# Attention scores computed in four token groups, one quarter of the TensorE array's columns each

## The chip, the core and the metric

The kernel runs on one core of one Trainium2 chip. A core has a matrix engine (TensorE, in the profile PE for matmuls and PEld for the loads of its stationary operand), a vector engine (VectorE, DVE), a scalar engine (ScalarE, ACT), GpSimd (POOL) and a queue that issues DMAs (SyncE, SP). They run at the same time and wait for each other by semaphores. Matmul results go to PSUM, which has eight banks of 512 fp32 numbers on each of 128 partitions. The metric is the device time of one execution in microseconds (us), lower is better.

## The reference, cut to what matters

The program is a recommendation tower. `r_x` (1024 tokens of 2048 numbers) goes through two encoders, and each gives four states of 512 numbers for a token. The change lies in the complex attention over these four states:

```python
B, IN, HID, D, N, OUT = (4096, 2048, 2048, 512, 4, 512)   # H = 8 heads, HD = 64
sr = enc(er_W1, ...)          # (tokens, N, D): layer norm, gelu, two matmuls
si = enc(ei_W1, ...)
qr = heads(sr @ Wq_r.T + bq_r);  qi = heads(si @ Wq_i.T + bq_i)
kr = heads(sr @ Wk_r.T + bk_r);  ki = heads(si @ Wk_i.T + bk_i)
vr = heads(sr @ Wv_r.T + bv_r);  vi = heads(si @ Wv_i.T + bv_i)
ar = einsum('bhnd,bhmd->bhnm', qr, kr) + einsum('bhnd,bhmd->bhnm', qi, ki)
ai = einsum('bhnd,bhmd->bhnm', qi, kr) - einsum('bhnd,bhmd->bhnm', qr, ki)
mag = sqrt(ar ** 2 + ai ** 2 + 1e-08) * HD ** (-0.5)
w = softmax(mag, axis=-1)
out_r = einsum('bhnm,bhmd->bhnd', w, vr) ...
out_i = einsum('bhnm,bhmd->bhnd', w, vi) ...
attn_r = out_r @ Wo_r.T + bo_r;  attn_i = out_i @ Wo_i.T + bo_i
```

So every token has, for each of the 8 heads, a 4 x 4 table of scores between its own four states, and nothing between one token and another. Behind it come an interaction, a measurement and a small MLP.

## The kernel before

Three large parts follow each other: the first layers of both encoders (to about 713 us of the profiled span), their second layers (to about 1397 us), and `phase_states`, which has the attention (about 1399 to 2330 us) and then the rest to the end.

The attention works on 16 blocks (`NB`) of 64 tokens (`BT`). A block has C = 256 columns, 4 states times 64 tokens, kept as NG = 2 groups of 128 columns; a group is 4 states (n) times GB = 32 tokens (b). The 8 heads are taken in KD = 4 pairs, index `m`; a pair has two heads `h`. For every `m` of a block, called a step below, these pieces are issued:

- `project` (PE): queries and keys, 48 matmuls 128x256 in a split of three products (lines 53 to 55).
- `q_evac` (ACT) and `k_evac` (DVE): copy them out of PSUM, with biases, into `qs` and `ks`. `ks` holds two parts, so that one matmul gives both `ar` and `ai`.
- `score` (PE, L2041): for each head and group one fp32 matmul, stationary `qs` of 128 columns, moving `ks` of 2 x 128 columns. Its result is 128 x 128 for `ar` and for `ai`: all pairs of the 32 tokens, of which only the pairs within one token are wanted. The trace has two load records and two matmul records for each fp32 matmul. The head `h` has its own PSUM bank.
- `t_square` (ACT, L1315): squares of a bank, 512 columns, once per head.
- `pick` (DVE, L1629, L1634, L1638): adds the squares of `ar` and `ai`, multiplies by `g.mask` (1 where the tokens agree), and sums over the tokens, which leaves 16 numbers per partition.
- `t_magnitude`, `shift`, `exponent`, `total`: the softmax, once a block.
- `spread` (DVE, L1668): writes the weights back into a 128 x 128 table that is zero between different tokens, `pd`, one for each of the GH = 4 pairs of head and group.
- `t_turn` (PE, L2051) transposes `pd`, `pt_evac` (ACT, L1321) copies the result to `ptl`, and `mix` (PE, L2062) multiplies it with the values; `o_high` and `o_low` read the mix.

Each engine's order is written out by hand in its own `block_body`. The softmax of a block is used one block later: in block b, PE issues for each `m` from 1 to 3 `project(b, m)`, `t_turn(b-1, m-1)`, `score(b, m-1)`, `mix(b-1, m-1)`. Thus `score` stands between the transposes and the mix, and ACT's `pt_evac` runs while PE does `score`. The last turn, score and mix of a block stand among the matmuls for the values, and `project_out` (lines 53 to 55 again, from `t_ohi`) follows. Blocks 0 and 1 are written out, 2 to 14 run in a loop on each engine, 15 is written out.

Of the kernel before, what the change touches and what calls it, by code (L numbers as in the profile page):

```python
# [9 lines left out]
ACT = mybir.ActivationFunctionType  # L10
ALU = mybir.AluOpType
# [16 lines left out]
GB = P // N  # L28
KI = IN // P
# [889 lines left out]
def phase_states(nc, g):  # L919
# [4 lines left out]
    GH = NG * 2  # L924
    NP = 8 * KD
# [9 lines left out]
    with s.ctx:  # L935
# [15 lines left out]
        sq = sb_t("sq", [P, 2, W])  # L951
        m2 = sb_t("m2", [P, W])
# [62 lines left out]
        scored = s.sem("t_scored")  # L1015
        t_squared = s.sem("t_squared")
# [282 lines left out]
        def _(act):  # L1299
            def q_evac(b, m):  # L1300
                if not isinstance(b, int) or 4 * b + m >= 2:
                    act.wait_ge(scored, b * 8 + (2 * m - 2))
# [7 lines left out]
            def t_square(b, m):  # L1310
                for h in range(2):
                    act.wait_ge(scored, b * 8 + (2 * m + h + 1))
                    if not isinstance(b, int) or 4 * b + m >= 1:
                        act.wait_ge(t_summed, b * 4 + m)
                    act.activation(sq[:, h, :], b_sc[:, h, :], ACT.Square).then_inc(t_squared, 1)  # L1315

            def pt_evac(b, m):
# [3 lines left out]
                act.activation(ptl[:, m % 2, :], pm(b, m), ACT.Copy).then_inc(pt_read, 1)  # L1321
# [290 lines left out]
        def _(dve):  # L1612
            def k_evac(b, m):
                if not isinstance(b, int) or 4 * b + m >= 2:
                    dve.wait_ge(scored, b * 8 + (2 * m - 2))
# [7 lines left out]
            def pick(b, m):  # L1623

                dve.wait_ge(t_squared, b * 8 + (2 * m + 2))
                if not isinstance(b, int) or 4 * b + m >= 1:
                    dve.wait_ge(picked, b * 4 + m)
                sqv = sq[:, :, :].rearrange("p h (a c) -> p a h c", a=2)
                dve.tensor_tensor(m2[:, :].rearrange("p (h c) -> p h c", h=2), sqv[:, 0], sqv[:, 1], ALU.add).then_inc(t_summed, 1)  # L1629

                sqv = m2[:, :].rearrange("p (g c) -> p g c", g=GH)
                mask = g.mask[:, :, :].rearrange("p n b -> p (n b)").unsqueeze(1).to_broadcast([P, GH, P])
                dve.wait_ge(t_summed, b * 4 + (m + 1))
                dve.tensor_tensor(sqv, sqv, mask, ALU.mult).then_inc(stepped, 1)  # L1634
                dve.wait_ge(stepped, b * 6 + (m + 1))
                if not isinstance(b, int) or b >= 1:
                    dve.wait_ge(t_mag_done, b)
                dve.tensor_reduce(mg2[:, m, :, :].rearrange("p g n -> p (g n)"),  # L1638
                                  m2[:, :].rearrange("p (x b) -> p x b", b=GB), AX.X, ALU.add).then_inc(picked, 1)
# [23 lines left out]
            def spread(b, m):  # L1663
# [3 lines left out]
                for x in range(GH):  # L1667
                    ins = dve.scalar_tensor_tensor(  # L1668
                        out=pd[:, x, :, :], in0=ex[:, m, x, :].unsqueeze(2).to_broadcast([P, N, GB]),
                        scalar=tinv[:, m, x:x + 1], in1=g.mask[:, :, :], op0=ALU.mult, op1=ALU.mult)  # L1670
# [33 lines left out]

            def block_body(b, first):
# [682 lines left out]
```

## Time and profile before

| | us |
|---|---|
| median of 3 runs (2923.43 to 2924.65) | 2924.25 |
| the profiled execution's own time | 2926.15 |
| its span | 2924.4 |
| PE busy | 2812.8 |
| PEld busy | 2433.5 |
| DVE busy | 2105.9 |
| ACT busy | 1326.4 |

The profiled execution is 1.9 us longer than the median, and its span leaves 1.75 us of it outside. Busy times of different engines overlap and don't add up. A PE record lasts longer than its share of the engine, since matmuls are pipelined: the distance from one record's start to the next is what a matmul costs in a row of them. Where the trace merges records, as "x8", the time shown runs from the first start to the last end.

### The profile page before, as it was taken

To read this page: it belongs to the slowest core of one execution; us is meant where nothing else is said; L and a number is where in the kernel's file an instruction comes from. 1 tells how busy PE (TensorE), PEld (TensorE's weight loads), DVE (VectorE), ACT (ScalarE), POOL (GpSimd) and SP (SyncE) were. 2 spreads that over 40 slices of the span, in tenths; PEclk is the share of its full clock that TensorE was granted. 3 is DMA by queue.
4 is the path that set the end of the run, shared out by engine and by line. 5 is a ranking of instruction groups with operands and counts; after the bars stand their busy time and mean duration, and the time that the engine had idled before them with its cause. 6 is when DMAs were issued, how large, how long until landed. Compare 5 with 4: busy or idle time off the path is not lost. (4 is left out here: it accounts for less than half of the span.)

```text
span 2924.4 us, 41074 instructions
## 1 busy us (share of the span) xinstructions
PE 2812.8 (96%) x15040; PEld 2433.5 (83%) x15040; DVE 2105.9 (72%) x3170; ACT 1326.4 (45%) x2000; POOL 140.1 (5%) x177
## 2 busy tenths in 40 slices
PE   8999999998999999999899999999999899999797
PEld 6888888887788877888899999999999877778686
DVE  5787778763658756688677667667766759999863
ACT  2232432243533244434455555555554655555543
POOL 1000000001001010010000001000000000000000
PEclk9999999999999999999999999999999999999899
DMA  6555565535737776378422322232223463344310
GB/s 240 192 202 187 180 219 183 199 141 180 238 125 246 248 267 209 123 268 284 161 59 73 91 67 58 73 99 58 57 86 86 117 157 94 93 110 122 109 37 11
DMA packets 493712, 420.36 MB, mean 144 GB/s; under 512 B 282272, under 2 KB 397088, under 8 KB 493344
## 3 DMA queue, kind: packets, MB, share of 16 engines
q1 hardware_dynamic: 459168, 341.20, 37.9%
q0 software_dynamic: 17792, 60.89, 5.5%
q10 hardware_dynamic: 16640, 16.78, 1.7%
q8 instruction: 70, 1.15, 0.2%
q14 instruction: 42, 0.34, 0.0%
HBM read 328.62 MB, written 90.18 MB: 143 GB/s over the span
## 5 line engine op out<-in xcount | busy, mean ns | idle before, releaser
L53 PE MATMUL banks<-a_hi 128*128 128x512 f32 x1024 | 399.7, 390 | 14.5 <-DVE a_lo L353 14.4
L54 PE MATMUL banks<-a_lo,a_hi 128*128 128x512 f32 x1024 | 399.2, 390 | 0.0
L55 PE MATMUL banks<-a_hi,a_lo 128*128 128x512 f32 x1024 | 399.1, 390 | 0.0
L53 PE MATMUL banks<-b_hi 128*128 128x512 f32 x896 | 357.0, 398 | 25.6 <-DVE b_lo L774 15.2
L54 PE MATMUL banks<-b_lo,b_hi 128*128 128x512 f32 x896 | 352.9, 394 | 0.0
L55 PE MATMUL banks<-b_hi,b_lo 128*128 128x512 f32 x896 | 352.5, 393 | 0.0
L53 PE MATMUL banks<-sx,g_hi 128*128 128x256 f32 x1024 | 293.4, 287 | 5.8 <-DMA sx<-s_scr 4.0
L55 PE MATMUL banks<-sx,g_lo 128*128 128x256 f32 x1024 | 290.5, 284 | 0.0
L54 PE MATMUL banks<-sx,g_hi 128*128 128x256 f32 x1024 | 290.4, 284 | 0.0
L1619 DVE TENSOR_SCALAR t_ks<-banks,cols 64x256 f32<-64x256 f32 x512 | 236.5, 482 | 55.4 <-PE banks L55 48.1
L53 PEld LDWEIGHTS banks<-a_hi 128*128 128x128 f32 x1024 | 192.7, 188 | 55.8 <-DVE a_lo L353 15.3
L53 PEld LDWEIGHTS banks<-b_hi 128*128 128x128 f32 x896 | 170.4, 190 | 67.9 <-DVE b_lo L774 30.8
L55 PEld LDWEIGHTS banks<-a_hi,a_lo 128*128 128x128 f32 x1024 | 192.8, 188 | 40.1
L54 PEld LDWEIGHTS banks<-a_lo,a_hi 128*128 128x128 f32 x1024 | 192.8, 188 | 39.8
L53 PE MATMUL banks<-g_hi,s_axng 128*128 128x512 f32 x512 | 203.9, 398 | 18.8 <-DVE s_cs L1769 14.6
L54 PE MATMUL banks<-g_lo,s_axng 128*128 128x512 f32 x512 | 202.9, 396 | 0.0
L53 PEld LDWEIGHTS banks<-sx,g_hi 128*128 128x128 f32 x1024 | 197.3, 193 | 6.5 <-DMA sx<-s_scr 4.2
L55 PE MATMUL banks<-g_hi,s_axng 128*128 128x512 f32 x512 | 202.5, 396 | 0.0
L55 PEld LDWEIGHTS banks<-b_hi,b_lo 128*128 128x128 f32 x896 | 170.6, 190 | 36.3
L54 PEld LDWEIGHTS banks<-b_lo,b_hi 128*128 128x128 f32 x896 | 170.8, 191 | 34.4
L54 PEld LDWEIGHTS banks<-sx,g_hi 128*128 128x128 f32 x1024 | 197.3, 193 | 0.1
L55 PEld LDWEIGHTS banks<-sx,g_lo 128*128 128x128 f32 x1024 | 197.1, 193 | 0.0
(199 smaller groups left out, 5820.4 us busy)
## 6 DMA issues: line engine op xcount, KB each, us to landing
w_ring<-w_first SPq DMA_DIRECT2D x192, 512.0 KB, 4.1
w_ring<-w_second SPq DMA_DIRECT2D x160, 512.0 KB, 4.7
sx<-s_scr SPq DMA_DIRECT2D x64, 512.0 KB, 4.4
a_scr<-t_at SPq DMA_DIRECT2D x256, 128.0 KB, 1.9
s_axng<-a_scr SPq DMA_DIRECT2D x64, 512.0 KB, 5.4
g_wraw<-w_pieces SPq DMA_DIRECT2D x74, 256.0 KB, 4.4
c<-h_scr ACTq DMA_DIRECT2D x16, 1024.0 KB, 6.8
w_ring<-w_second SPq DMA_DIRECT2D x64, 256.0 KB, 5.0
```

The lines of the kernel that those rows point to most:

```text
L53: mm(out, ahi, bhi, start=first, stop=False, **more)
L54: mm(out, ahi, blo, start=False, stop=False, **more)
L55: return mm(out, alo, bhi, start=False, stop=last, **more)
L1619: ins = dve.tensor_scalar(ks[half(at_half), m % 2, h, part, :], b_k[half(h), m % 2, e * C:(e + 1) * C], bcol(M_K + e, m, half(h)), float(s ...
```

## The change

A group's 32 tokens are cut into SG = 4 sets of SB = 8 tokens, token b going to set b mod 4. For each head and group, `score` issues four matmuls, one per set: 32 stationary columns (4 states of 8 tokens) and 2 x 32 moving columns, both read with a step of four fp32 numbers (16 bytes). The compiled instruction has a tile of 128 rows by 32 columns, at column 0, 32, 64 or 96 of the array, and writes 32 PSUM partitions. So all of a step's scores, both heads, take 256 columns of one bank; the bank alternates with `m`. The squares, the sum and the masked sum work on 256 and 128 columns where they had 2 x 512 and 512. Two small masks, `same` (the token within its set of eight) and `spot` (where a token stands in `pd`), are made once from the identity by two reductions. Since the rows of `pd` now stand in the order of the sets, `pt_evac` writes its result with a step of four numbers, which puts them back.

```diff
--- before.py
+++ after.py
@@ -26,6 +26,7 @@
 PARTITION = 224 * 1024 - 32
 BT = 64
 GB = P // N
+SB = 8
 KI = IN // P
 KD = D // P
 CHUNKS_A = 2 * HID // W + 1
@@ -922,6 +923,8 @@
     C = N * BT
     NG = BT // GB
     GH = NG * 2
+    SG = GB // SB
+    SC = N * SB
     NP = 8 * KD
     M_Q, M_K, M_V, M_O = 0, 2, 4, 6
     LAST_B = NB - 1
@@ -948,8 +951,10 @@
         qs = sb_t("qs", [P, 2, 2, C])
         ks = sb_t("ks", [P, 2, 2, 2, C])
         v = sb_t("v", [P, NG, H, 2, HD])
-        sq = sb_t("sq", [P, 2, W])
-        m2 = sb_t("m2", [P, W])
+        sq = sb_t("sq", [P, 2, GH, SC])
+        m2 = sb_t("m2", [P, GH, SC])
+        same = sb_t("same", [P, SB])
+        spot = sb_t("spot", [P, GB])
         pd = sb_t("pd", [P, GH, N, GB])
         ptl = sb_t("ptl", [P, 2, W])
         ohi = sb_t("ohi", [P, KD, 2, C], F32R)
@@ -1013,6 +1018,7 @@
         v_full = s.sem("t_v_full")
         v_read = s.sem("t_v_read")
         scored = s.sem("t_scored")
+        masks = s.sem("t_masks")
         t_squared = s.sem("t_squared")
         t_summed = s.sem("t_summed")
         stepped = s.sem("t_stepped")
@@ -1299,7 +1305,7 @@
         def _(act):
             def q_evac(b, m):
                 if not isinstance(b, int) or 4 * b + m >= 2:
-                    act.wait_ge(scored, b * 8 + (2 * m - 2))
+                    act.wait_ge(scored, b * 4 + (m - 1))
                 act.wait_ge(projected, b * 8 + (2 * m + 1))
                 for e in range(2):
                     for h in range(2):
@@ -1308,17 +1314,18 @@
                     ins.then_inc(q_read, 1)
 
             def t_square(b, m):
-                for h in range(2):
-                    act.wait_ge(scored, b * 8 + (2 * m + h + 1))
-                    if not isinstance(b, int) or 4 * b + m >= 1:
-                        act.wait_ge(t_summed, b * 4 + m)
-                    act.activation(sq[:, h, :], b_sc[:, h, :], ACT.Square).then_inc(t_squared, 1)
+                act.wait_ge(scored, b * 4 + (m + 1))
+                if not isinstance(b, int) or 4 * b + m >= 1:
+                    act.wait_ge(t_summed, b * 4 + m)
+                act.activation(sq[:, :, :, :].rearrange("p a g c -> p (a g c)"), b_sc[:, m % 2, 0:2 * GH * SC],
+                               ACT.Square).then_inc(t_squared, 1)
 
             def pt_evac(b, m):
                 act.wait_ge(p_turned, b * 4 + (m + 1))
                 if not isinstance(b, int) or 4 * b + m >= 2:
                     act.wait_ge(mixed, b * 4 + (m - 1))
-                act.activation(ptl[:, m % 2, :], pm(b, m), ACT.Copy).then_inc(pt_read, 1)
+                act.activation(ptl[:, m % 2, :].rearrange("p (x c s) -> p x s c", x=GH, s=SG),
+                               pm(b, m).rearrange("p (x s c) -> p x s c", x=GH, s=SG), ACT.Copy).then_inc(pt_read, 1)
 
             def o_high(b, m):
                 act.wait_ge(mixed, b * 4 + (m + 1))
@@ -1612,7 +1619,7 @@
         def _(dve):
             def k_evac(b, m):
                 if not isinstance(b, int) or 4 * b + m >= 2:
-                    dve.wait_ge(scored, b * 8 + (2 * m - 2))
+                    dve.wait_ge(scored, b * 4 + (m - 1))
                 dve.wait_ge(projected, b * 8 + (2 * m + 2))
                 for h in range(2):
                     for e, part, at_half, sign in K_PARTS:
@@ -1622,21 +1629,18 @@
 
             def pick(b, m):
 
-                dve.wait_ge(t_squared, b * 8 + (2 * m + 2))
+                dve.wait_ge(t_squared, b * 4 + (m + 1))
                 if not isinstance(b, int) or 4 * b + m >= 1:
                     dve.wait_ge(picked, b * 4 + m)
-                sqv = sq[:, :, :].rearrange("p h (a c) -> p a h c", a=2)
-                dve.tensor_tensor(m2[:, :].rearrange("p (h c) -> p h c", h=2), sqv[:, 0], sqv[:, 1], ALU.add).then_inc(t_summed, 1)
-
-                sqv = m2[:, :].rearrange("p (g c) -> p g c", g=GH)
-                mask = g.mask[:, :, :].rearrange("p n b -> p (n b)").unsqueeze(1).to_broadcast([P, GH, P])
+                dve.tensor_tensor(m2[:, :, :], sq[:, 0, :, :], sq[:, 1, :, :], ALU.add).then_inc(t_summed, 1)
+
+                terms = m2[:, :, :].rearrange("p g (n b) -> p (g n) b", n=N)
                 dve.wait_ge(t_summed, b * 4 + (m + 1))
-                dve.tensor_tensor(sqv, sqv, mask, ALU.mult).then_inc(stepped, 1)
+                dve.tensor_tensor(terms, terms, same[:, :].unsqueeze(1).to_broadcast([P, GH * N, SB]), ALU.mult).then_inc(stepped, 1)
                 dve.wait_ge(stepped, b * 6 + (m + 1))
                 if not isinstance(b, int) or b >= 1:
                     dve.wait_ge(t_mag_done, b)
-                dve.tensor_reduce(mg2[:, m, :, :].rearrange("p g n -> p (g n)"),
-                                  m2[:, :].rearrange("p (x b) -> p x b", b=GB), AX.X, ALU.add).then_inc(picked, 1)
+                dve.tensor_reduce(mg2[:, m, :, :].rearrange("p g n -> p (g n)"), terms, AX.X, ALU.add).then_inc(picked, 1)
 
             def shift(b):
                 dve.wait_ge(t_mag_done, b + 1)
@@ -1667,7 +1671,7 @@
                 for x in range(GH):
                     ins = dve.scalar_tensor_tensor(
                         out=pd[:, x, :, :], in0=ex[:, m, x, :].unsqueeze(2).to_broadcast([P, N, GB]),
-                        scalar=tinv[:, m, x:x + 1], in1=g.mask[:, :, :], op0=ALU.mult, op1=ALU.mult)
+                        scalar=tinv[:, m, x:x + 1], in1=spot[:, :].unsqueeze(1).to_broadcast([P, N, GB]), op0=ALU.mult, op1=ALU.mult)
                 ins.then_inc(pd_made, 1)
 
             def o_low(b, m):
@@ -1702,10 +1706,18 @@
                 c = g.c22[:, i, :]
                 dve.tensor_tensor(c.bitcast(F32R), c, f32(last_home(i)), ALU.subtract).then_inc(last_split, 1)
 
+            def masks_made():
+
+                dve.tensor_reduce(same[:, :], g.ident[:, :].rearrange("p (j b) -> p b j", b=SB), AX.X, ALU.add).then_inc(masks, 1)
+                dve.tensor_reduce(spot[:, :].rearrange("p (j s) -> p s j", s=SG),
+                                  g.ident[:, :].rearrange("p (s n j) -> p s j n", n=N, s=SG), AX.X, ALU.add).then_inc(masks, 1)
+
             def block_body(b, first):
                 if first:
                     for i in range(4):
                         last_low(i)
+                    masks_made()
+                    dve.wait_ge(masks, 2)
                 k_evac(b, 0)
                 for m in range(1, KD):
                     if not first:
@@ -2032,14 +2044,17 @@
                 pe.wait_ge(q_read, b * 8 + (2 * m + 2))
                 for h in range(2):
                     pe.wait_ge(k_read[h], b * 4 + (m + 1))
+                if not isinstance(b, int) or 4 * b + m >= 2:
+                    pe.wait_ge(t_squared, b * 4 + (m - 1))
+                bank = b_sc[:, m % 2, 0:2 * GH * SC].rearrange("p (a x c) -> p a x c", a=2, x=GH)
                 for h in range(2):
-                    if not isinstance(b, int) or 4 * b + m >= 1:
-                        pe.wait_ge(t_squared, b * 8 + (2 * m - 1 + h))
                     for gr in range(NG):
                         cols = slice(gr * P, (gr + 1) * P)
-                        out = b_sc[:, h, :].rearrange("p (a g c) -> p a g c", a=2, g=NG)[:, :, gr]
-                        mm = pe.matmul(out, qs[:, m % 2, h, cols], ks[:, m % 2, h, :, cols], start=True, stop=True)
-                    mm.then_inc(scored, 1)
+                        q = qs[:, m % 2, h, cols].rearrange("p (c s) -> p s c", s=SG)
+                        k = ks[:, m % 2, h, :, cols].rearrange("p a (c s) -> p s a c", s=SG)
+                        for sg in range(SG):
+                            mm = pe.matmul(bank[sg * SC:(sg + 1) * SC, :, h * NG + gr], q[:, sg], k[:, sg], start=True, stop=True)
+                mm.then_inc(scored, 1)
 
             def t_turn(b, m):
                 pe.wait_ge(pd_made, b * 4 + (m + 1))
```

On PE, this is a step inside the loop over blocks, with what the instructions wait for. Before (`t_pd` is read by the transposes, `t_qs` and `t_ks` by `score`, `t_ptl` by `mix`):

```order
L55 MATMUL banks<-sx,g_lo 128x256
L2051 MATMUL banks<-ident,t_pd 128x128 [waits s_t_pd_made]
L2051 MATMUL banks<-ident,t_pd 128x128 x3
L2041 MATMUL banks<-t_ks,t_qs 128x2x128 [waits s_t_k_read1,s_t_squared,s_t_k_read0,s_t_q_read]
L2041 MATMUL banks<-t_ks,t_qs 128x2x128
L2041 MATMUL banks<-t_ks,t_qs 128x2x128 [waits s_t_squared]
L2041 MATMUL banks<-t_ks,t_qs 128x2x128
L2062 MATMUL banks<-t_ptl,t_v 128x128 [waits s_t_v_read,s_t_pt_read]
L2062 MATMUL banks<-t_ptl,t_v 128x128 x3
```

And in the changed kernel:

```order
L56 MATMUL banks<-sx,g_lo 128x256
L2066 MATMUL banks<-ident,t_pd 128x128 [waits s_t_pd_made]
L2066 MATMUL banks<-ident,t_pd 128x128 x3
L2056 MATMUL banks<-t_ks,t_qs 32x2x32 [waits s_t_k_read1,s_t_squared,s_t_k_read0,s_t_q_read]
L2056 MATMUL banks<-t_ks,t_qs 32x2x32 x15
L2077 MATMUL banks<-t_ptl,t_v 128x128 [waits s_t_v_read,s_t_pt_read]
L2077 MATMUL banks<-t_ptl,t_v 128x128 x3
```

Four matmuls became 16, in the same place between the transposes and the mix, and the second wait for the squares is gone.

On ACT, the evacuation of the transposes and the squares of the same kind of step stood before as:

```order
L1321 ACTIVATE t_ptl<-banks 128x512 [waits s_t_mixed,s_t_p_turned]
L1315 ACTIVATE t_sq<-banks 128x512 [waits s_t_summed,s_t_scored] x2
L1330 ACTIVATE t_ohi<-banks,cols 64x256 [waits s_t_mixed]
```

and stand now as:

```order
L1327 ACTIVATE t_ptl<-banks 128x4x4x32 [waits s_t_mixed,s_t_p_turned]
L1320 ACTIVATE t_sq<-banks 128x256 [waits s_t_summed,s_t_scored]
L1337 ACTIVATE t_ohi<-banks,cols 64x256 [waits s_t_mixed]
```

One square of 256 columns takes the place of two of 512, and the copy to `t_ptl` has four dimensions.

## Rows read from the trace of the kernel before

**Rows 1.** The page's first part, and the granted clock of its second.

```profile
PE 2812.8 (96%) x15040; PEld 2433.5 (83%) x15040; DVE 2105.9 (72%) x3170; ACT 1326.4 (45%) x2000; POOL 140.1 (5%) x177
PEclk9999999999999999999999999999999999999899
```

**Rows 2.** Windows, the attention and some of it: length, busy by engine, clock, DMA.

```profile
1399.00:2330.00 931.00, 917.20 (x6560) 870.51 (x6559) 656.78 (x1537) 503.13 (x973) 37.06 (x42) 0.99 0.29 81
...
1450.00:1520.00 70.00, 70.00 (x505) 66.99 (x505) 49.10 (x116) 36.61 (x73) 0.00 (x0) 0.98 0.23 61
```

**Rows 3.** Waits of PE in the attention: total us, times, longest.

```profile
PE banks L2051 <- DVE t_pd L1668: 6.3, 1, 6.3
...
PE banks L2041 <- DVE t_ks L1619: 0.7, 1, 0.7
```

**Rows 4.** Groups by shape, PE, the attention: count, busy us, mean ns, idle.

```profile
L2041 PE MATMUL banks<-t_ks,t_qs 128*128 128x256 f32 x512 | 121.2, 379 | 0.7 <-DVE t_ks L1619 0.7
...
L2062 PE MATMUL banks<-t_ptl,t_v 128*128 128x128 f32 x512 | 69.0, 279 | 0.0
L2051 PE MATMUL banks<-ident,t_pd 128*128 128x128 f32 x256 | 38.9, 275 | 6.3 <-DVE t_pd L1668 6.3
```

**Rows 5.** Timeline, one step in the loop: start us, us, engine, work, idle before.

```profile
1708.45 0.60 PE L2051 MATMUL banks<-ident,t_pd 128*128 128x128 f32 x4
1708.78 1.60 PEld L2041 LDWEIGHTS banks<-t_ks,t_qs 128*128 128x128 f32 x8
1708.89 1.89 PE L2041 MATMUL banks<-t_ks,t_qs 128*128 128x256 f32 x8
...
1709.09 0.60 ACT L1321 ACTIVATE t_ptl<-banks 128x512 f32<-128x512 f32 x1 [1.39 <-PE banks L2051]
...
1710.03 0.60 ACT L1315 ACTIVATE t_sq<-banks 128x512 f32<-128x512 f32 x1 [0.35 <-PE banks L2041]
1710.40 1.08 PEld L2062 LDWEIGHTS banks<-t_ptl,t_v 128*128 128x128 f32 x8
1710.62 1.05 PE L2062 MATMUL banks<-t_ptl,t_v 128*128 128x128 f32 x8
...
1710.82 0.60 ACT L1315 ACTIVATE t_sq<-banks 128x512 f32<-128x512 f32 x1 [0.19 <-PE banks L2041]
...
1711.43 0.48 PE L53 MATMUL banks<-g_hi,sx 128*128 128x512 f32 x1
```

**Rows 6.** Groups by shape, DVE and ACT, in the attention (1400 to 2330 us).

```profile
L1629 DVE TENSOR_TENSOR t_m<-t_sq 128x512 f32<-128x512 f32 x64 | 44.3, 693 | 22.2 <-ACT t_sq L1315 20.7
L1634 DVE TENSOR_TENSOR t_m<-t_m,mask 128x512 f32<-128x512 f32 x64 | 44.3, 692 | 2.2
L1638 DVE TENSOR_REDUCE t_mg<-t_m 128x16 f32<-128x512 f32 x64 | 43.9, 686 | 2.2
...
L1648 DVE TENSOR_TENSOR t_dif<-t_mag,t_top 128x64 f32<-128x64 f32 x16 | 3.6, 226 | 0.5
L1655 DVE TENSOR_REDUCE t_tot<-t_ex 128x16 f32<-128x64 f32 x16 | 3.5, 221 | 7.4 <-ACT t_ex L1352 7.4
...
L1315 ACT ACTIVATE t_sq<-banks 128x512 f32<-128x512 f32 x128 | 76.4, 597 | 44.3 <-PE banks L2041 44.1
...
L1352 ACT ACTIVATE t_ex<-t_dif 128x64 f32<-128x64 f32 x16 | 4.1, 256 | 0.2
```

**Rows 7.** Timeline, the first block: DVE's first key copies and PE's first score.

```profile
1407.27 7.60 DVE L1619 TENSOR_SCALAR t_ks<-banks,cols 64x256 f32<-64x256 f32 x16
...
1411.19 1.97 PE L2041 MATMUL banks<-t_ks,t_qs 128*128 128x256 f32 x8 [0.66 <-DVE t_ks L1619]
```

**Rows 8.** Timeline, the last block: what ACT does ahead of the magnitudes.

```profile
2303.13 0.60 ACT L1338 ACTIVATE t_v<-banks 128x512 f32<-128x512 f32 x1 [1.96 <-PE banks L55]
...
2303.75 1.28 ACT L1345 ACT_TABLE_LOAD   x1
```

## Prediction, on record before the changed kernel ran

> **What bounds the kernel now.** I read the page's busy times first: PE is busy 96% of the span, DVE 72%, ACT 45%, and PE's granted clock stays at nine tenths or more in all slices but one, which shows eight: the 2.4 GHz level throughout [rows 1]. The windows say the same of the attention alone: PE is busy 917.2 of 931 us, and in a stretch inside the loop over blocks 70.00 of 70.00, while DVE has 49 and ACT 37 of these 70 us [rows 2]. The waits of PE confirm it: in the whole attention it waits once for `pd` (6.3 us) and once for a key copy (0.7 us), and never for a square or for `ptl` [rows 3]. So what the change takes off DVE and ACT is worth nothing by itself, and what it does to PE between the transposes and the mix counts in full, 64 times (16 blocks of 4 steps).
>
> Next the group of the scores: 512 matmul records for 256 matmuls, two records each [rows 4]. The timeline of one step shows what they cost: the first score record starts at 1708.89, the first mix record at 1710.62, so `score` holds PE for 1.73 us [rows 5]. Eight records in 1.89 us, the last of them 0.38 long, start (1.89 - 0.38) / 7 = 0.216 us apart. Each streams 256 columns. The eight mix records of 128 columns start (1.05 - 0.28) / 7 = 0.110 us apart [rows 4, 5]. Hence 0.106 us for 128 columns more, or 0.83 ns a column, and about 4 ns beside it.
>
> **The change, part by part.**
>
> The scores on PE. Taken away: 4 matmuls, 8 records, 1.73 us a step. Added: 16 matmuls, 32 load records and 32 matmul records, each of 2 x 32 = 64 columns. Their columns add up to 32 x 64 = 2048, as 8 x 256 did: the work that is dropped is in the width of the stationary operand, 32 instead of 128, and a matmul's time in rows 5 goes by its moving columns. So if the four quarters of the array work one after the other, nothing is saved. The price of a record of 64 columns stands nowhere in the trace. By the line above it is 0.110 - 64 x 0.00083 = 0.057 us, and 32 of them take 1.83 us.
>
> To that comes the change of the array's shape, twice a step, which the trace doesn't show either. Now the load for the scores starts at 1708.78, 0.27 ahead of the transposes' end at 1709.05, and the load for the mix at 1710.40, just as the last of the eight score records starts [rows 5]: each group's weights are loaded under the group before. A record lasts 0.379 us where they start 0.216 apart, so 0.163 us of it is the way through the array [rows 4, 5]. I let this become visible once on entering and once on leaving, 0.33 us. It may be nothing (if the next shape's weights go in under the old one), or some 0.5 with a load of 0.11 exposed at either end.
>
> A step's scores then take 1.83 + 0.33 = 2.16 us, 0.43 more than now; times 64 that is 27.5 us. The ends for this term are wide. Below: four quarters side by side, and nothing for the shape, leaves at least what the copy to `ptl` needs. It runs from 1709.09 to 1709.69, 0.80 us behind the first score record [rows 5], and the mix reads it: 0.80 - 1.73 = -0.93 a step, -60 us. Above: each of the 32 pairs of load and matmul costs as much as the cheapest pairs of the trace, the 128-column ones at 0.110 us: 3.52 + 0.33 - 1.73 = 2.12 a step, +136 us. I take the value by streamed columns, because the two rows of scores and mix lie on a line that has almost no constant part; nothing in them shows a smallest price, but neither does anything there go below 0.110.
>
> The Trainium skill (TensorEngine Tiling (Array Packing), Key Properties) says that changing the tiling mode drains the engine; no run here shows it so far. By that rule the 0.33 us above, which comes from rows, is kept rather than dropped; without it the change would cost +6 instead of +27 us.
>
> The same engine's waits. `score` waited twice for squares, once per bank; now once, for those of two steps back. Neither is seen among PE's waits [rows 3], so this gives nothing.
>
> ACT. Per step two squares of 512 columns, 0.597 each, become one of 256, which lies between 0.256 (64 columns) and 0.597 [rows 6]; some 0.4, so about 0.8 us less a step. The copy to `ptl` writes with a step of four numbers. If this doubled its 0.60 us it would end at 1710.29, ahead of the load for the mix at 1710.40 [rows 5]; with scores of 2.16 us the cover grows by 0.4. Cost nothing. If the scores got shorter than about 1.3 us a doubled copy would show.
>
> DVE. The three passes of `pick` take 0.693, 0.692 and 0.686 for 512 columns; at 64 columns such passes take 0.226 and 0.221 [rows 6], so at 128 about 0.29 each: 1.2 us less a step, under PE's work. `spread` has the same shape and count, with another table.
>
> The masks. Two reductions of 128 elements, about 0.29 each by the same line, stand ahead of DVE's first key copy. DVE is occupied without a gap from 1407.27 on, and PE's first score already waits 0.66 us for these copies [rows 7]. So they push PE: +0.6 us, once (between 0.4 and 1.4, the latter with both as long as a 512-column pass).
>
> The end of the last block. Here PE waits 6.3 us for `pd`, and one might hope for the shorter squares and sums ahead of the softmax. But ACT sits idle 1.96 us for the values on PE, copies them, and only then loads its table for the magnitudes [rows 8]: the squares were done before. This wait moves with PE's work and gives nothing.
>
> **Sum.** 64 x 0.43 + 0.6 = +28 us. Against the profiled execution, 2926.15, that is 2954; this execution stands 1.9 us over the median of the runs, so the forecast for the median is 2924.25 + 28 = 2952 us, 1% slower. Its own range, with the shape change at nothing and at 0.5 to 0.6 each step plus a few ns a record: +7 to +55, that is 2931 to 2979.
>
> **Rivals.**
>
> A, the quarters work side by side, and the kernel is faster. The 16 matmuls go to the four quarters in turn, so the next one's first record needn't wait for the last one's second. The two records of one matmul do use the same quarter and follow each other, and records start in order, so one matmul per 0.057 us is what I expect: 16 x 0.057 = 0.91, with the 0.33 of the shape 1.24 us, 0.49 less than now. Times 64 and with the masks: -31 us, 2893. For it: PE's loads already run ahead and under matmuls, 66.99 of 70 us of load beside 70 of matmul [rows 2]; DVE and ACT both have room for a step shortened by half a microsecond. Against it: no record pair in the trace is less than 0.110 apart, and every one is full-width, so that two matmuls streaming at once is something no row shows. The Trainium skill (TensorE: Matmul & The Clock Gate, Part 3) tells of three column tiles of 512 columns running 2.38 times as fast as in a row, which is why this case has a large chance; its example is eight times as long as a record here.
>
> B, a small matmul has a price of its own, and the kernel is much slower. With 0.110 us for each pair: +136 us, 3061. The same sum comes out if the operands' step of four numbers halves the rate of the stream, since a record would then stream 64 columns in the time of 128. For it: 0.110 is the least in the trace, and no operand of a matmul there is read with such a step. Against it: the load of 128 columns alone could set this 0.110, and the loads here have 32. The Trainium skill (SBUF — State Buffer, the note on cachelines) speaks for it: full rate wants at least two accesses in a line of 16 bytes, and each access here is in a new line; by that rule the time would be near 3061 too if the stream is what sets the time, and under A's overlap near no change.
>
> C, the change does nothing that can be measured. Somewhere between A and the forecast the two effects cancel: scores of 1.64 to 1.82 us a step. The issue of 64 load and matmul instructions in a row would do that at 0.026 to 0.028 us each. No row gives such a price, and the window is narrow.
>
> **How the numbers follow.** Forecast 0.47, A 0.34, B 0.12, C 0.07. Of 0.2% (about 5.8 us, which is what a measurement of this kernel can tell from no change), the forecast and B lie above and A below. A could be smaller than worked out, but still outside 5.8 us unless it is C. So slower 0.58, same 0.07, faster 0.35. The range takes in A's value and reaches over the forecast to part of the way to B: 2889 to 3000. Below it is A with nothing for the shape change (0.08), above it most of B (0.12).
>
> **What would show it.** In the profile after: the group of score records (1024 matmul records, some perhaps missing) with their distance in the timeline of one step. About 0.057 apart is the forecast, four or so within 0.06 and their pieces overlapping is A, 0.1 or more is B. The distances from the start of the last transpose record to that of the first score record, and from the last score record to the first mix record, give the price of the shape change; they are 0.11 and 0.22 now, and I expect 0.16 more in each, less what a shorter record takes off the second. PE's waits should name neither `ptl` nor squares; if `ptl` from ACT turns up there, the scores are shorter than the copy and A holds with its floor. The windows of the other parts, before 1399 and after the attention, should be as long as before. PE's busy share can't tell these cases apart, the length of the attention can: 931 us now, 959 by the forecast, 900 by A, 1067 by B. If that length changes without the distance from first score to first mix changing, my account of PE as the sole bound is wrong.

## The result, and the profile after

The changed kernel takes 2907.06 us (median of 4 runs, 2903.67 to 2908.35) beside 2924.45 us before (4 runs, 2923.43 to 2927.56): a ratio of 0.9937, with a 95% interval of 0.992 to 0.9954. That is 17.4 us less, where I had forecast 28 more. The prediction was wrong in its sign; the outcome lies on the side of rival A, at 56% of its size.

The page's busy times, the attention (931 us before) and the waits of PE there, which answer to [rows 1 to 3]. The columns of the second are length, busy by engine, clock and DMA:

```profile
PE 2784.5 (96%) x16576; PEld 2392.7 (82%) x16576; DVE 2031.9 (70%) x3172; ACT 1306.5 (45%) x1936; POOL 139.9 (5%) x177
```

```profile
1399.00:2312.00 913.00, 890.97 (x8087) 830.27 (x8086) 583.07 (x1538) 481.42 (x904) 37.12 (x42) 0.99 0.30 82
```

```profile
PE banks L2066 <- DVE t_pd L1672: 6.2, 1, 6.2
...
PE banks L2077 <- ACT t_ptl L1327: 3.4, 13, 0.3
```

The window's end was set by me, 18 us earlier than before, so its length shows nothing. Two fixed points do: PE's first record of the attention, and its last group of transposes, which waits for `pd`. Before:

```profile
1398.80 0.36 PE L53 MATMUL banks<-sx,g_hi 128*128 128x256 f32 x1 [1.80 <-PEq L517]
...
2324.88 1.12 PE L2051 MATMUL banks<-ident,t_pd 128*128 128x128 f32 x4 [6.31 <-DVE t_pd L1668]
```

After:

```profile
1398.65 0.36 PE L54 MATMUL banks<-sx,g_hi 128*128 128x256 f32 x1 [1.80 <-PEq L518]
...
2309.63 1.11 PE L2066 MATMUL banks<-ident,t_pd 128*128 128x128 f32 x4 [6.23 <-DVE t_pd L1672]
```

That is 926.1 us before and 911.0 after, 15.1 less. The other 3 us of the profiled spans' difference lie behind it (599.5 us to the end before, 596.6 after), where the change does nothing. That part varies between 594.9 and 601.0 us over all 14 traces, so these 3 us can't be put down to the change. PE's busy share can't show any of this, as it is 96% both times.

There is a new name among the waits: the mix (L2077) waits for the copy to `ptl`. The 3.4 us are only what is visible as idle PE; most of it hides under the end of the last score record, whose 0.3 us are mostly the way through the array. The 13 visible waits are those of the first step in each of the 13 blocks that run in the loop.

One step in the loop, the timeline (start us, us, engine, work, idle before it), to be read beside [rows 5]:

```profile
1703.63 0.60 PE L2066 MATMUL banks<-ident,t_pd 128*128 128x128 f32 x4
1704.16 0.90 PEld L2056 LDWEIGHTS banks<-t_ks,t_qs 128*32 128x32 f32 x32 [0.17 <-issue]
1704.16 1.17 PE L2056 MATMUL banks<-t_ks,t_qs 128*32 128x64 f32 x32
1704.27 1.12 ACT L1327 ACTIVATE t_ptl<-banks 128x512 f32<-128x512 f32 x1 [1.39 <-PE banks L2066]
...
1705.39 0.38 ACT L1320 ACTIVATE t_sq<-banks 128x256 f32<-128x256 f32 x1
1705.44 0.97 PEld L2077 LDWEIGHTS banks<-t_ptl,t_v 128*128 128x128 f32 x8 [0.38 <-ACT t_ptl L1327]
1705.44 1.16 PE L2077 MATMUL banks<-t_ptl,t_v 128*128 128x128 f32 x8
...
1706.35 0.48 PE L54 MATMUL banks<-g_hi,sx 128*128 128x512 f32 x1
```

Three distances between starts say where the time went:

| from the start of | before | after |
|---|---|---|
| transposes to scores | 0.44 | 0.53 |
| scores to mix | 1.73 | 1.28 |
| mix to the next projection | 0.81 | 0.91 |
| sum | 2.98 | 2.72 |

So this step is 0.26 us shorter. Not every step gains as much: in the first step of each block in the loop, scores to mix takes 1.42 to 1.46 us instead of 1.27 to 1.31. One of them:

```profile
1743.64 1.17 PE L2056 MATMUL banks<-t_ks,t_qs 128*32 128x64 f32 x32
1745.07 1.15 PE L2077 MATMUL banks<-t_ptl,t_v 128*128 128x128 f32 x8 [0.26 <-ACT t_ptl L1327]
```

There the copy starts 0.12 us behind the transposes' end instead of 0.04, and the mix 0.13 behind the copy's end instead of 0.05; no run here shows why. Over the 60 steps that have transposes, scores and mix the mean gain is 0.22 us, 13.0 us in all. The four groups of scores of the first block, which no mix follows, give 2.2 more, and 0.7 is lost to the masks (below): 14.5 of the 15.1 us.

The copy to `ptl` has grown to 1.12 us and ends at 1705.39; the mix starts at 1705.44, right behind it. The 32 score records start (1.17 - 0.30) / 31 = 0.028 us apart on average, half of my 0.057. They don't start evenly. The timeline of the same step, cut off at 1704.28 and at 1704.40, has four records and then eight:

```profile
1704.16 0.34 PE L2056 MATMUL banks<-t_ks,t_qs 128*32 128x64 f32 x4
```

```profile
1704.16 0.46 PE L2056 MATMUL banks<-t_ks,t_qs 128*32 128x64 f32 x8
```

Four records start within 0.02 us, then PE starts none for about 0.1 us, then the next four. Over all 64 steps the distance from one four to the next is 0.121 us. A record doesn't name its quarter, but the matmuls go to the four quarters in turn and the records come in fours, so I read it as all four quarters at work at once, with a record of 64 columns taking 0.121 us in each.

The groups of ScalarE and VectorE, as in [rows 6], and the first of the two masks:

```profile
L1327 ACT ACTIVATE t_ptl<-banks 128x512 f32<-128x512 f32 x64 | 71.7, 1121 | 125.2 <-PE banks L2066 125.2
...
L1320 ACT ACTIVATE t_sq<-banks 128x256 f32<-128x256 f32 x64 | 24.5, 383 | 13.9 <-PE banks L2056 13.3
```

```profile
L1635 DVE TENSOR_TENSOR t_m<-t_sq 128x128 f32<-128x128 f32 x64 | 18.7, 293 | 32.3 <-ACT t_sq L1320 30.8
...
L1643 DVE TENSOR_REDUCE t_mg<-t_m 128x16 f32<-128x128 f32 x64 | 18.3, 286 | 2.2
...
L1711 DVE TENSOR_REDUCE t_same<-ident 128x8 f32<-128x128 f32 x1 | 0.4, 393 | 0.0
```

The first score, as in [rows 7]:

```profile
1411.79 1.17 PE L2056 MATMUL banks<-t_ks,t_qs 128*32 128x64 f32 x32 [1.38 <-DVE t_ks L1626]
```

PE waits 1.38 us for the key copies where it waited 0.66: the masks push it by 0.7.

### The profile page after: what moved, and what is told of

It reads as the page before. It is cut to its first block and busy times, and to the rows that moved or that the text cites. A ratio compares the mean times of both kernels' runs of the same rounds, so it can differ in the third digit from the quotient of the medians.

```text
span 2906.2 us, 43956 instructions
## 1 busy us (share of the span) xinstructions
PE 2784.5 (96%) x16576; PEld 2392.7 (82%) x16576; DVE 2031.9 (70%) x3172; ACT 1306.5 (45%) x1936; POOL 139.9 (5%) x177
```

## The experiments

Five questions were left. Is it the overlap of the quarters that makes the records cheap? What does the way into and out of their shape cost? What did the stepped copy take back? Does the 16-byte step of the operands matter? Did the relief of VectorE and ScalarE give anything?

Several kernels were timed in one run only. Their traces carry the comparison: the length from PE's first record of the attention to its last group of transposes, as above, is 926.1, 925.6 and 926.0 us in the three kernels whose PE work is that of before (before, e4, e12), and so repeats within 0.5 us.

| kernel | us | against |
|---|---|---|
| changed | 911.0 | before -15.1 |
| e1 | 898.5 | changed -12.5 |
| e2 | 988.1 | e1 +89.6 |
| e3 | 905.7 | e1 +7.2 |
| e5 | 879.9 | e1 -18.7 |
| e6 | 910.7 | e2 -77.4 |
| e7 | 960.0 | e1 +61.5 |
| e8 | 1043.2 | before +117.1 |
| e9 | 879.5 | e1 -19.0 |
| e10 | 879.8 | e9 +0.3 |
| e11 | 894.2 | e1 -4.3 |

### e1: the transposes put the tokens in order, the copy has no step

```diff
-  act.activation(ptl[...].rearrange("p (x c s) -> p x s c", ...), pm(b, m).rearrange(...), ACT.Copy)
+  act.activation(ptl[:, m % 2, :], pm(b, m), ACT.Copy)
+  # once: reid, the identity with its columns in the order of the tokens
+  dve.tensor_copy(reid[:, :].rearrange("p (c s) -> p c s", s=SG), g.ident[:, :].rearrange("p (s c) -> p c s", s=SG))
-  pe.transpose(..., pd[:, x, :, :].rearrange("p n b -> p (n b)"), g.ident[:, :])
+  pe.transpose(..., pd[:, x, :, :].rearrange("p n b -> p (n b)"), reid[:, :])
```

> The changed kernel, with the rows of pd put back in order by the transposes (they multiply with a reordered identity) and the copy to ptl written without a step. Theory 1: the stepped copy (1.12 us instead of 0.60) has taken the place of the scores as what the mix waits for; with it back at 0.60 the mix follows the last score record, first score to first mix falls from 1.28 to about 1.1 us, the mix's loads run ahead again (another 0.1), so 0.2 to 0.28 us a step less, 64 times: 13 to 18 us under the changed kernel, about 2891. Theory 2: the way out of the 32-column tiles costs that time anyway (the last score record ends 0.11 us ahead of the first mix record), so no more than 3 us are gained, about 2905.

Measured: 2897.46 us (ratio to before 0.9902, 0.9886 to 0.9919), 9.6 under the changed kernel.

```profile
1693.28 0.60 PE L2068 MATMUL banks<-t_reid,t_pd 128*128 128x128 f32 x4
...
1693.81 1.17 PE L2058 MATMUL banks<-t_ks,t_qs 128*32 128x64 f32 x32
1693.91 0.60 ACT L1328 ACTIVATE t_ptl<-banks 128x512 f32<-128x512 f32 x1 [1.39 <-PE banks L2068]
...
1694.91 0.97 PEld L2079 LDWEIGHTS banks<-t_ptl,t_v 128*128 128x128 f32 x8 [0.20 <-issue]
1694.91 1.16 PE L2079 MATMUL banks<-t_ptl,t_v 128*128 128x128 f32 x8
...
1695.83 0.36 PE L54 MATMUL banks<-sx,g_hi 128*128 128x256 f32 x1
```

Neither theory has it whole. The copy is at 0.60 again, ends at 1694.51, and nothing waits for it; scores to mix is 1.10 instead of 1.28, in the first steps of the loop's blocks too, and the attention is 12.5 us shorter. But the mix's loads don't run ahead again: the load of the mix starts with its first matmul, and mix to projection stays at 0.92. So that tenth of a microsecond, and the one ahead of the scores (still 0.53), belong to the change of shape and not to the copy.

### e2: four matmuls of one quarter in a row

```diff
-  for h in range(2): for gr in range(NG): ... for sg in range(SG):
+  for sg in range(SG): for h in range(2): for gr in range(NG):
```

> As e1, with the same 16 score matmuls in another order: the four of one quarter of the columns one after another, then the next quarter. Theory A (quarters stream side by side, one quarter can't): 13 of 16 matmuls then cost two records of 64 columns in a row, 0.11 us, instead of 0.057, so the scores take about 1.6 us from first to last record instead of 0.87, some 0.7 us a step more, 45 us over e1. Theory B (a record of this size costs its load of 32 columns, 0.028 us, wherever it goes): the same time as e1 within 2 us.

Measured: 2985.99 us, 88.5 more than e1, from the order of the same 16 matmuls alone.

```profile
1728.25 2.61 PE L2058 MATMUL banks<-t_ks,t_qs 128*32 128x64 f32 x32
1730.79 1.16 PE L2079 MATMUL banks<-t_ptl,t_v 128*128 128x128 f32 x8
```

The records start (2.61 - 0.30) / 31 = 0.0745 us apart on average instead of 0.028, and scores to mix is 2.54 instead of 1.10 us. The overlap of different quarters is shown.

The average mixes two things. Here are the first four records, all of one quarter:

```profile
1728.25 0.67 PE L2058 MATMUL banks<-t_ks,t_qs 128*32 128x64 f32 x4
```

They start 0.133 and then 0.118 us apart, which is the 0.12 that a quarter takes for a record in the changed kernel too. Where the order passes from one quarter to the next, records come in pairs, about 0.118 us from pair to pair. I read them as the last four of one quarter beside the first four of the next. So 32 records take 20 such places, where in turn they take 8.

### e3: ar and ai apart

```diff
-  mm = pe.matmul(bank[..., :, h * NG + gr], q[:, sg], k[:, sg], ...)
+  for a in range(2): mm = pe.matmul(bank[..., a, h * NG + gr], q[:, sg], k[:, sg, a], ...)
```

> As e1, with each score matmul cut into two of 32 moving columns (ar and ai apart): 32 matmuls, 64 load and 64 matmul records, as many streamed columns as before. Theory A (streaming sets the time, two quarters at once): from first to last record about 0.9 to 1.0 us, as in e1, total within 5 us of e1. Theory B (each load-and-matmul pair has a price of 0.028 us): 64 x 0.028 = 1.8 us, 0.9 us a step more, about 58 us over e1.

Measured: 2904.32 us (one run), 6.9 more than e1 (7.2 in the attention) and far from 58.

```profile
1693.81 1.38 PE L2059 MATMUL banks<-t_ks,t_qs 128*32 128x32 f32 x64
```

64 records of 32 columns start (1.38 - 0.24) / 63 = 0.018 us apart. A record of this engine can therefore be much cheaper than the 0.110 that was the least in the trace of before, and what sets the time is nearer to the streamed columns than to the number of records.

### e4: the shorter squares and sums alone, in the kernel before

```diff
-  act.activation(sq[:, h, :], b_sc[:, h, :], ACT.Square)
+  act.activation(sq[:, h, 0:P], b_sc[:, h, 0:P], ACT.Square)      # pick: three passes on 128 columns
```

> The kernel before, with only the work of ScalarE and VectorE shortened as in the change: two squares of 128 columns and the three passes of the pick on 128 columns; the squares and sums of the other columns are left out. Theory 1 (PE alone sets the time in the attention): 2924 us, within 3 us of before. Rival (part of the gain came from the relief of VectorE and ScalarE): 5 to 17 us under before.

Measured: 2925.13 us beside 2925.53 before (0.9997, 0.9988 to 1.0007), with VectorE's busy time in the attention down to that of the changed kernel.

```profile
1399.00:2330.00 931.00, 917.45 (x6555) 870.75 (x6553) 583.67 (x1539) 462.72 (x975) 37.10 (x42) 0.99 0.29 81
```

73 us of VectorE's work and 40 of ScalarE's are gone against [rows 2], PE's work is the same, and the attention is as long as before within 0.5 us. That half of the change is worth nothing here.

### e5 and e6: neighbouring columns, the quarters in turn and in a row

```diff
-  q = qs[:, m % 2, h, cols].rearrange("p (c s) -> p s c", s=SG)
-  k = ks[:, m % 2, h, :, cols].rearrange("p a (c s) -> p s a c", s=SG)
+  q = qs[:, m % 2, h, cols].rearrange("p (s c) -> p s c", s=SG)
+  k = ks[:, m % 2, h, :, cols].rearrange("p a (s c) -> p s a c", s=SG)
```

> As e1, but each score matmul reads 32 neighbouring columns for both operands instead of every fourth (so it computes the scores between tokens of one state alone; those between different states are left out). Theory S (the step of 16 bytes slows load or stream, and the overlap of quarters only hides some of it): records closer than 0.028 us, the step's scores 0.1 us or more shorter, 6 us or more under e1. Theory N (the step costs nothing): the spacing of e1 and its 2897 us within 3.

> As e2 (four matmuls of one quarter one after another), with neighbouring columns as in e5 (scores between different states are left out). In e2 the 32 records start 0.0745 us apart, more than the 0.057 that streamed columns give. Theory S: the step of 16 bytes is what lies between; 0.057 here, 0.55 us a step less, about 35 us under e2, 2951. Theory L (in one quarter the load of 32 columns isn't hidden under the stream before it, as it is in the full array): 0.0745 again and 2986 within 3.

The edit is shown against e1 for e5 and against e2 for e6.

Measured: 2875.81 us for e5 and 2909.47 for e6 (one run each), 21.7 under e1 and 76.5 under e2 (18.7 and 77.4 in the attention).

Of e5:

```profile
1693.38 0.65 PE L2058 MATMUL banks<-t_ks,t_qs 128*32 128x64 f32 x32
1694.13 1.16 PE L2079 MATMUL banks<-t_ptl,t_v 128*128 128x128 f32 x8
```

Of e6, all its records and the first four of them:

```profile
1701.90 1.39 PE L2058 MATMUL banks<-t_ks,t_qs 128*32 128x64 f32 x32
```

```profile
1701.90 0.41 PE L2058 MATMUL banks<-t_ks,t_qs 128*32 128x64 f32 x4
```

The average spacing falls from 0.028 to (0.65 - 0.22) / 31 = 0.0139 in turn, and from 0.0745 to (1.39 - 0.22) / 31 = 0.0377 in a row: by the same factor of two both times. In one quarter alone it is 0.118 with the step (e2) and 0.056 without (e6, behind a first distance of 0.080). In turn, four records start every 0.121 us with the step (e1) and every 0.056 without (e5). So the step of four numbers halves the rate, at either order, which is the second mechanism I had named under rival B. The Trainium skill (SBUF — State Buffer, the note on cachelines) says that full rate wants two accesses to a line of 16 bytes; these runs agree, with the numbers just given.

In e5 the gain doesn't come out whole. The last score record starts 0.43 us behind the first, but the mix waits for the copy to `ptl`, which even without a step ends 0.70 behind it; scores to mix is 0.75.

### e7: every score matmul twice

```diff
-  for sg in range(SG):
+  for sg in tuple(range(SG)) * 2:
```

> As e1, with every score matmul issued twice: 32 instead of 16. It gives the price of one matmul, and by subtraction what the change of shape costs. If 16 matmuls cost 16 x 0.056 = 0.90 us (spacing of e1) the time is 58 us over e1, 2955, and of the 1.10 us from first score to first mix 0.2 us are the way out of the shape. Rival: the first matmuls cost more than the later ones (queue filling), and the second 16 add clearly less, under 45 us.

Measured: 2960.38 us, 62.9 over e1 (ratio to before 1.0123, 1.0106 to 1.014). The rival, that the first matmuls cost more than the later ones, is out: it wanted under 45.

```profile
1703.17 2.14 PE L2058 MATMUL banks<-t_ks,t_qs 128*32 128x64 f32 x64
1705.23 1.16 PE L2079 MATMUL banks<-t_ptl,t_v 128*128 128x128 f32 x8
```

16 more matmuls cost 62.9 / 64 = 0.98 us a step, 0.061 each. Of e1's 1.10 us from scores to mix 0.12 are then not matmuls. With 0.09 more ahead of the scores and 0.10 more behind the mix's start, the change of shape costs 0.31 us a step, 20 us in all.

### e8: 64 moving columns in the full array

```diff
-  mm = pe.matmul(out, qs[:, m % 2, h, cols], ks[:, m % 2, h, :, cols], ...)
+  for j in range(4): c = slice(j * 32, (j + 1) * 32)
+      mm = pe.matmul(out[:, :, c], qs[:, m % 2, h, cols], ks[:, m % 2, h, :, cols][:, :, c], ...)
```

> The kernel before, full array, with each score matmul cut into four of 64 moving columns: 16 matmuls, 32 records, each with its load of 128 stationary columns. Theory 1 (the 0.110 us of the 128-column pairs in the trace of before was their load's, so it says nothing of a 32-column load): the records start 0.107 to 0.11 us apart, 3.5 us a step, 1.75 more than before, 112 us more: 3037. Theory 2 (it was the stream's): 0.057 apart, 7 us more: 2932.

Measured: 3045.91 us (one run), 121 over before (117 in the attention, where 112 was expected).

```profile
1694.88 3.68 PE L2043 MATMUL banks<-t_ks,t_qs 128*128 128x64 f32 x32
```

(3.68 - 0.27) / 31 = 0.110 us apart, as for 128 columns. In the full array the moving columns don't set this price. The load of 128 stationary columns, which all these records share, is the likely reason; no run tells it from another fixed price of a full-width record. So the mix's 0.110, the second of the two points through which I had laid my line, needn't be stream time. It happens to lie where the stream alone would put it, at half of the 0.216 for 256 columns.

### e9 and e10: the scores of e5, complete

The copies out of PSUM write queries and keys set by set, in runs of eight numbers; each matmul reads 32 neighbouring columns.

```diff
-  act.activation(qs[half(e), m % 2, h, :], b_q[half(h), e * C:(e + 1) * C], ...)
+  act.activation(in_sets(qs[half(e), m % 2, h, :]), by_eight(b_q[half(h), e * C:(e + 1) * C]), ...)
+  # by_eight: "p (x s j) -> p x s j", in_sets: "p (s x j) -> p x s j", j = 8; the same for ks on VectorE
-  q[:, sg], k[:, sg]
+  qs[:, m % 2, h, cols], ks[:, m % 2, h, :, cols]     # cols: 32 neighbours, from (sg * NG + gr) * 32
```

Left out here: `spot` and the reordered identity of e1 follow the new order. e10 leaves the keys in their old order and reads the moving operand in runs of eight.

> As e1, but the copies of queries and keys out of PSUM write them set by set (tokens 8s to 8s+7 are set s, in runs of eight numbers), so that each score matmul reads 32 neighbouring columns and all scores are computed. Theory 1 (e5's gain is the matmul's reading, and copies in runs of 8 cost ScalarE and VectorE nothing): e5's 2876 us within 4. Theory 2 (writing in runs is slowed as the copy to ptl was by its step, 1.9 times): the four query copies take 3.6 instead of 1.9 us, delay the copy to ptl behind them, and the mix waits; 2885 or more.

> As e9, but the keys are stored in their old order and the matmul reads its moving operand in runs of eight neighbouring numbers. If only the 16-byte step costs and a run of eight reads at full rate: the time of e9 within 3 us. If every break in the addresses costs: 5 us or more over e9.

Measured: e9 2877.48 us (ratio to before 0.9835, 0.9821 to 0.9849), e10 2874.62 (one run).

One step of e9:

```profile
1692.33 0.60 PE L2073 MATMUL banks<-t_reid,t_pd 128*128 128x128 f32 x4
...
1692.86 0.65 PE L2062 MATMUL banks<-t_ks,t_qs 128*32 128x64 f32 x32
1692.96 0.60 ACT L1334 ACTIVATE t_ptl<-banks 128x512 f32<-128x512 f32 x1 [1.39 <-PE banks L2073]
...
1693.61 0.97 PEld L2084 LDWEIGHTS banks<-t_ptl,t_v 128*128 128x128 f32 x8 [0.26 <-ACT t_ptl L1334]
1693.61 1.16 PE L2084 MATMUL banks<-t_ptl,t_v 128*128 128x128 f32 x8
```

The query copies, in the same execution:

```profile
L1319 ACT ACTIVATE t_qs<-banks,cols 64x256 f32<-64x256 f32 x256 | 120.1, 469 | 114.7 <-PE banks L56 111.5
```

They last 469 ns as before: runs of eight cost the writer nothing, where a step of four numbers cost it a factor of 1.9. Scores to mix is 0.75 us, and the mix now follows the unstepped copy to `ptl`. This version is 48.7 us under before and about 30 under the changed kernel.

Since the mix waits for the same copy in e5, e9 and e10, their times can't show whether e10's moving operand is read at the full rate. Its score records can:

```profile
1694.19 0.65 PE L2063 MATMUL banks<-t_ks,t_qs 128*32 128x64 f32 x32
```

They take 0.65 us, as in e5 and e9.

### e11: the step on the moving operand alone

```diff
-  q = qs[:, m % 2, h, cols].rearrange("p (c s) -> p s c", s=SG)
+  q = qs[:, m % 2, h, cols].rearrange("p (s c) -> p s c", s=SG)
```

> As e1, with neighbouring columns for the stationary operand and every fourth for the moving one (the scores it computes mix the wrong tokens). It splits e5's 22 us. If the load is what the step slows: near e5, 2876. If the stream is: near e1, 2897.

Measured: 2893.26 us (one run), 4.2 under e1 and 17.5 over e5 (4.3 and 14.4 in the attention).

```profile
1697.35 1.12 PE L2058 MATMUL banks<-t_ks,t_qs 128*32 128x64 f32 x32
```

(1.12 - 0.29) / 31 = 0.027 apart, and 0.117 us from four to four where e1 has 0.121 and e5 0.056. It is the stream that the step slows; the load's part is small while the stream has its step too. The load's step alone was not run.

### e12: the stepped copy in the kernel before

```diff
-  act.activation(ptl[:, m % 2, :], pm(b, m), ACT.Copy)
+  act.activation(ptl[...].rearrange("p (x c s) -> p x s c", x=4, s=4), pm(b, m).rearrange(...), ACT.Copy)
```

> The kernel before, with the copy to ptl written with a step of four numbers as in the change (so the weights reach the mix in the wrong order). By my prediction: the copy doubles to about 1.1 us, ends ahead of the mix's loads under 1.73 us of scores, and costs nothing, 2924 within 3 us. Rival: the step delays the squares behind it on ScalarE or disturbs PE, 5 us or more over before.

Measured: 2922.60 us beside 2926.21 (0.9987, 0.9978 to 0.9997).

```profile
1691.41 1.89 PE L2042 MATMUL banks<-t_ks,t_qs 128*128 128x256 f32 x8
1691.69 1.10 ACT L1321 ACTIVATE t_ptl<-banks 128x512 f32<-128x512 f32 x1 [1.46 <-PE banks L2052]
```

The copy takes 1.10 us and ends at 1692.79, under scores that last to 1693.14. The 3.6 us are on the other side of a cost, and they aren't in the attention, which is 926.0 us long beside 926.1. The copy costs nothing where the scores take 1.73 us, and 0.18 us a step (more in the first step of a block) where they take 1.1: the same copy, with and without its cover.

## Why the prediction was wrong

**The step that failed** is the assumption "if the four quarters of the array work one after the other": a record of 64 columns every 0.057 us, 1.83 us for 32. They work side by side, four records at a time, and the 32 records take 0.87 us from the first start to the last. e2 shows that the order over the quarters is the cause, since with the same matmuls in another order the forecast's sign would have come true, at twice its size.

**The price of 0.057** was itself right for one quarter: 0.056 in e6, where neighbouring columns are read. Since a record there costs no more than its streamed columns do by the rows of before, the load of 32 columns between two records takes no visible time. With the change's step of 16 bytes the price is 0.12. So the forecast had two terms wrong, in opposite directions: the overlap, worth a factor of four, and the step, worth a factor of two. With the quarters one after the other, as the forecast has it, the step would have made the 32 records cost some 3.8 us and not 1.83 (an estimate, 32 times the 0.118 of e2), a little over rival B's 3.52.

**Rival A** had the right direction and 0.91 us for the scores, near the 0.87 measured, but by another way: it let one matmul of two records start every 0.057 us, two quarters at a time, and four records start every 0.121. The deeper overlap and the halved rate nearly cancel, so its agreement is luck. The sign that I had written down for it, four or so within 0.06, came, but each four is followed by a pause; only in e5, e9 and e10 does the next four follow after 0.056. A said -31 us and -17 came. The difference is 0.23 us a step: its sum of 1.24 stands against 1.28 + 0.09 + 0.10 = 1.47. Of that, 0.18 is the wait for the stepped copy. I had given the condition ("shorter than about 1.3 us a doubled copy would show") and not carried it into A's sum, where the scores were 1.24.

**Rival B**: the general price of 0.110 per pair was wrong (0.018 in e3). The halving by the 16-byte step was right (e5, e6), mostly by the stream (e11), and hidden under A's overlap only in part: 22 us lay in it, with the copy to `ptl` as the next limit. I had put "near no change" for the two together, and they gave -17.

**The change of shape**: 0.33 us taken, 0.31 measured, in three pieces of which I had foreseen two, each at 0.16 (0.09 and 0.12 came); the third is the mix's loads, which no longer run ahead (e1). That the sum agrees is in part luck. The rule of the Trainium skill that a change of tiling mode drains the engine (TensorEngine Tiling (Array Packing), Key Properties) agrees with the 0.17 and 0.20 us that the loads wait for nothing visible at either end; a drain itself isn't a row of the trace. What the rows show is less overlap: the first score record starts 0.07 us ahead of the end that the profile gives the transposes, where it was 0.16 before.

**The rest held.** PE alone sets the time in the attention: the shorter steps, less the masks, are 14.5 of the 15.1 us, and VectorE's and ScalarE's relief is worth nothing (e4). The copy doubled and would have been covered at 1.73 us (e12). Passes at 128 columns took 0.29 us as estimated, the square 0.38. The masks cost 0.7 where I said 0.6. The wait at the end of the last block stayed at 6.2 us. The prediction took the two waits in [rows 3] for all of PE's in the attention; the trace of before has four more (4.0 us for a DMA of `sx`, and 1.8, 1.7 and 0.5), none of them for a square or for `ptl`, so nothing hangs on it.

The range held the result, near its lower end, without the mechanism. What misled the forecast was to count the absence of overlap in the trace as evidence against it, though no row before could have shown any: all its matmuls use the whole array.

## What to carry to other kernels

A matmul with a narrow stationary operand gained nothing here by its width alone (e2's attention is 62 us longer than before); it gains when neighbours in the order go to different column quarters (e1 against e2, 88 us), and when each operand lies in neighbouring numbers (e5 against e1, 22 us). Let the copy out of PSUM write the operand in the order in which it will be read, in runs of eight numbers, the one length tried here (e9). When a stage on the critical engine is shortened, the price of every piece that it covered has to be put into that same sum.

## What the runs showed that I had not expected

- With 128x32 tiles of the array in turn, records of 64 fp32 columns start four at a time: every 0.056 us with neighbouring columns (e5), every 0.121 with columns 16 bytes apart (e1). Within a four they start 0.007 us apart.
- A matmul that reads fp32 numbers 16 bytes apart runs at half rate: 0.028 against 0.0139 us a record in turn, 0.0745 against 0.0377 in a row. In runs of eight it reads at full rate (e10: 32 records in 0.65 us, as in e5).
- ScalarE writes fp32 with a step of 16 bytes at 1.12 us per 128x512, and 0.597 without. It writes runs of eight (64x256) at the 469 ns of the plain form.
- A transpose on TensorE with a reordered identity gives the reordered transpose at the same 0.60 us for four, so a permutation within a transposed tile is free (e1).
- A group in another shape costs 0.31 us on the way in and out together, 0.10 of it in the matmuls after it.
